# Stacking DMAs of an attention layer: rows interleaved by four, one key stack whole-width, one issued by GpSimd

## The reference

```python
def _L1_gnn_ref(x, adj_matrix, bond_matrix, Wq, bq, Wk, bk, Wv, bv, Wo, bo, seq_len):
    q, k, v = (proj(Wq, bq), proj(Wk, bk), proj(Wv, bv))
    scores = jnp.einsum('bhqd,bhkd->bhqk', q, k) * SCALE
    mask = (adj_matrix + bond_matrix)[:, None, :, :]
    scores = scores * mask
    attn = jax.nn.softmax(scores, axis=-1)
    ctx = jnp.einsum('bhqk,bhkd->bhqd', attn, v)
    ctx = ctx.transpose(0, 2, 1, 3).reshape(b, seq_len, EMBED_DIM)
    return jnp.einsum('bse,fe->bsf', ctx, Wo) + bo
```

## Time and profile before

| | |
|---|---|
| median of 3 runs | 3081.29 us (3079.47 to 3081.74) |
| the profiled execution | 3079.83 us |
| its span | 3078.0 us |
| mean granted clock of TensorE | 0.993 |
| TensorE busy | 2976.1 us (97%) |
| VectorE, ScalarE, GpSimd busy | 61%, 48%, 23% |
| DMA queue of SP | 98576 packets, 199.96 MB |

### The profile page before, as it was taken

One profiled execution on the slowest core, in us unless ns is written; L12 is line 12 of the kernel. 1 busy time (PEld: TensorE's weight loads), 2 busy tenths in 40 slices (PEclk: granted clock), 3 DMA queues, 4 the chain that ended last, 5 costly groups with the idle time before them and its releaser, 6 DMA issues.

```text
span 3078.0 us, 63372 instructions
## 1 busy us (share of the span) xinstructions
PE 2976.1 (97%) x22896; PEld 2353.4 (76%) x22896; DVE 1893.0 (61%) x4170; ACT 1473.6 (48%) x2729; POOL 692.9 (23%) x1241
## 2 busy tenths in 40 slices
PE   7999999999999999999999999999999999999999
PEld 6687786877878777788777887778867788677886
DVE  2698426984269742787437874378643786438863
ACT  1684217833178331783327833277322773238722
POOL 0243002430024300242002420034200342013410
PEclk9999999999999999999999999999999999999999
DMA  4302213022130231302313013121132212221200
GB/s 169 90 2 90 76 70 90 2 90 86 59 90 2 90 108 44 84 3 89 131 30 75 19 73 131 39 66 45 58 119 53 52 59 66 97 67 38 80 8 14
DMA packets 98905, 204.35 MB, mean 66 GB/s; under 512 B 11024, under 2 KB 42128, under 8 KB 98576
## 3 DMA queue, kind: packets, MB, share of 16 engines
q1 hardware_dynamic: 98576, 199.96, 20.9%
HBM read 136.75 MB, written 8.65 MB: 47 GB/s over the span
## 4 chain that ended last, share of the span: by engine, by line
PE 68%; issue 11%; DVE 8%; SPq 5%; POOL 4%; ACT 3%; DMA 1%; DVEq 0%; POOLq 0%; ACTq 0%
PE ps L1077 37%; PE ps L1300 11%; PE ps L1224 7%; SPq L446 4%; PE ps L1372 4%; PE ps L1252 4%; PE ps L1202 3%; POOL H L557 3%; DVE Z L787 2%; DVE stats L608 1%; DVE h L845 1%; PE ps L1114 1%; POOL nm L545 1%; ACT Z L1002 1%; DMA qS<-qlo 1%
## 5 line engine op out<-in xcount | busy, mean ns | idle before, releaser
L787 DVE CUSTOM_DVE_ANT_0 Z<-ps,adjN 128x1024 f32<-128x1024 f32 x512 | 623.8, 1218 | 69.9 <-PE ps L1202 69.9
L1002 ACT ACTIVATE Z<-Z,nm 128x1024 f32<-128x1024 f32 x512 | 587.1, 1147 | 66.7 <-POOL nm L545 66.7
L1224 PE MATMUL ps<-ident,Z 128*128 128x128 f32 x4096 | 547.8, 277 | 26.5 <-ACT Z L1002 17.6
L1224 PEld LDWEIGHTS ps<-ident,Z 128*128 128x128 f32 x4096 | 459.7, 141 | 139.3 <-issue 64.1
L1202 PE MATMUL ps<-kS,qS 128*128 128x512 f32 x1024 | 372.1, 446 | 28.4 <-DMA qS<-qlo 28.4
L534 POOL TENSOR_SCALAR ve<-mv 128x4 f32<-128x4 f32 x80 | 15.7, 196 | 1340.1 <-DVE mv L613 1339.4
L557 POOL TENSOR_SCALAR H<-adjN 128x128 fp32r<-128x128 f32 (+1 forms) x456 | 316.8, 695 | 0.0
L545 POOL TENSOR_TENSOR nm<-nm,minus 128x1 f32<-128x1 f32 x512 | 97.1, 190 | 767.4 <-DVE nm L787 762.8
L1077 PE MATMUL ps<-mh,adjT 128*128 128x256 f32 x1024 | 223.6, 379 | 0.0
L1077 PE MATMUL ps<-v,P 128*128 128x257 f32 x1024 | 223.6, 379 | 0.0
L1077 PE MATMUL ps<-hT,t3T 128*128 128x512 f32 x512 | 221.0, 592 | 0.0
(11 more groups left out here) (170 smaller groups left out, 5673.5 us busy)
## 6 DMA issues: line engine op xcount, KB each, us to landing
adjT<-adjT_in SPq DMA_DIRECT2D x8, 4096.0 KB, 13.1
adjN<-adj_in SPq DMA_DIRECT2D x8, 4096.0 KB, 17.3
adjT<-adjT_in SPq DMA_DIRECT2D x8, 2048.0 KB, 9.1
qS<-qhi SPq DMA_DIRECT2D x112, 128.0 KB, 2.5
qS<-qlo SPq DMA_DIRECT2D x112, 128.0 KB, 2.5
kS<-khi SPq DMA_DIRECT2D x96, 128.0 KB, 2.4
kS<-klo SPq DMA_DIRECT2D x96, 128.0 KB, 2.5
adjT<-adjT_in SPq DMA_DIRECT2D x8, 1536.0 KB, 12.0
```

What stands on the lines that cost most here:

```text
L787: dve.tensor_tensor_reduce(Z[:, u % ZS], ps[:, 2 * (u % 2):2 * (u % 2) + 2].rearrange("p a n -> p (a n)"), adjN[:, u // HEADS], SCORE_SCAL ...
L1002: act.activation(Z[:, u % ZS], Z[:, u % ZS], ACT.Exp, bias=nm[:, u:u + 1], accum_out=sm[:, u:u + 1]).then_inc(exps.sem, 1)
L1224: mm = pe.transpose(ps[:, turn_bank((u, s)), rows(a)], Z[:, u % ZS, rows(NT // 2 * s + a)], ident[:])
```

## The change

Three things. The rows of q and k on the partitions are interleaved: partition 4c + j of a group's tile holds column c of the group's j-th head, where it was partition 32j + c. The host permutes weights and biases accordingly, and `pick` and `stack` step by four partitions. Then k(0,2) and k(1,2) become one stack of all 1024 columns, four DMAs with one semaphore (`kS_in[0][2]`; there is none for half 1). And k(1,1) leaves SP's queue; GpSimd issues it after its addition to x, once five lower parts are there, before `negate_max(0)`. `stack` takes the issuing queue as an argument.

```diff
-        kS_in = [[signal(f"kS_in{s}{j}", 64) for j in range(HPG - 1)] for s in range(NH)]
+        kS_in = [[signal(f"kS_in{s}{j}", 64) for j in range(HPG - 1 - s)] for s in range(NH)]
...
+        def stack(queue, dst, parts, j, cols, done):
+
+            for r, src in enumerate(parts):
+                to = dst[r:P:HPG].rearrange("p (g j) n -> p g j n", j=HPG)[:, :, j, cols]
+                queue.dma_start(to.bitcast(F32), src[j:P:HPG, :, cols].bitcast(F32)).then_inc(done.sem, 16)
...
-                def stack(dst, parts, j, cols, done):
-
-                    for r, src in enumerate(parts):
-                        to = dst[HD * r:HD * r + HD].rearrange("p (g j) n -> p g j n", j=HPG)[:, :, j, cols]
-                        sp.dma_start(to.bitcast(F32), src[HD * j:HD * j + HD, :, cols].bitcast(F32)).then_inc(done.sem, 16)
-
                 def stack_k(s, j):
-                    stack(kS, (khi, khi, klo, klo), j, half(s), kS_in[s][j])
+                    stack(sp, kS, (khi, khi, klo, klo), j, half(s), kS_in[s][j])
...
                 stack_q(0, 0)
-                stack_k(1, 1)
                 stack_q(0, 1)
-                stack_k(0, 2)
-                stack_k(1, 2)
+                stack(sp, kS, (khi, khi, klo, klo), HPG - 2, slice(0, N), kS_in[0][HPG - 2])
                 stack_q(0, 2)
...
                 pool.tensor_tensor(x[:], x[:], bo1B[:].unsqueeze(1).broadcast_to([P, NT, D]), ALU.add).then_inc(xbo.sem, 1)
+                pool.wait_ge(*lo_s(b, 5))
+                stand(pool, waited_pool)
+                stack(pool, kS, (khi, khi, klo, klo), 1, half(1), kS_in[1][1])
...
-                    dve.tensor_scalar(pick[:, i, HD * r:HD * (r + 1)], ident[:, P - HD:P], float(r in blocks), None,
+                    dve.tensor_scalar(pick[:, i, r:P:HPG], ident[:, HPG - 1:P:HPG], float(r in blocks), None,
...
-                            pe.wait_ge(*kS_in[s][j](b, 64))
+                            if j < len(kS_in[s]):
+                                pe.wait_ge(*kS_in[s][j](b, 64))
...
+    def interleaved(a):
+
+        a = np.asarray(a)
+        return np.swapaxes(a.reshape(-1, P // 32, 32), -1, -2).reshape(a.shape)
...
-        "wq1": T(L1_gnn_Wq), "wk1": T(L1_gnn_Wk), "wv1": T(L1_gnn_Wv),
+        "wq1": interleaved(T(L1_gnn_Wq)), "wk1": interleaved(T(L1_gnn_Wk)), "wv1": T(L1_gnn_Wv),
...
-        "bq1": columns(L1_gnn_bq), "bk1": columns(L1_gnn_bk),
+        "bq1": columns(interleaved(L1_gnn_bq)), "bk1": columns(interleaved(L1_gnn_bk)),
```

More of the change, by code:

```diff
@@ L439, in batch @@
             def batch(b, last):
-                def stack(dst, parts, j, cols, done):
-                    for r, src in enumerate(parts):
-                        to = dst[HD * r:HD * r + HD].rearrange("p (g j) n -> p g j n", j=HPG)[:, :, j, cols]
-                        sp.dma_start(to.bitcast(F32), src[HD * j:HD * j + HD, :, cols].bitcast(F32)).then_inc(done.sem, 16)
                 def stack_k(s, j):
-                    stack(kS, (khi, khi, klo, klo), j, half(s), kS_in[s][j])
+                    stack(sp, kS, (khi, khi, klo, klo), j, half(s), kS_in[s][j])
                 def stack_q(s, j):
-                    stack(qS, (qhi, qlo, qhi, qlo), j, half(s), qS_in[s][j])
+                    stack(sp, qS, (qhi, qlo, qhi, qlo), j, half(s), qS_in[s][j])
                 sp.wait_ge(*lo_s(b, 2))
```

## The result

The changed kernel takes **3037.05 us** (median; 3035.89 to 3037.51), the kernel before 3080.85 beside it: ratio 0.9858, 95% interval 0.9841 to 0.9875. That is 43.8 us less, 5.5 us a batch, where 28.4 were forecast; the low end of the stated range was 3047. The direction was right and the size was not.

The account below looks back on a forecast made before the run. The prediction took SP's issuing queue at the head of each batch's layer 1 as the bound; removing TensorE's two waits saves 28.4 us over eight batches, 3079.8 to 3051.4, or 3053 us as a median; range 3047 to 3085.

Parts of the forecast that it names:

- Both waits: TensorE idle 1.66 us before unit 4's scores and 2.10 us before unit 6's, first batch's layer 1; both to go.
- the sum: Profiled execution 3079.8 us less 28.4 is 3051.4, or 3053 us on the scale of the median.
- Rows interleaved: Stacking DMAs touch partitions all over instead of 32 in a block; could give transfer rate, taken as no change.
- Two queues on one set of engines: GpSimd's four DMAs could make q(0,0) land about 0.55 us later; charged nothing, at most 0.6 us in one batch.
- GpSimd's price: Time of one DMA issue of k(1,1) on GpSimd: taken as 1.0 us, bounds 0.60 and 4.53 us.
- free limit of 1.36: Four GpSimd issues before unit 0's negated maximum are free up to 5.4 us in all, 1.36 us each.
- (a): GpSimd's issue is the new bound, delaying unit 0's exponential beyond 1.36 us each; 3098 us at 2.77; slower, chance 0.17.
- (b): A GpSimd issue near 1.8 us costs 1.8 us a batch, 3067 us; chance 0.10.
- The whole-width stack: Third key stack in four DMAs at 0.60 us per issue: another 2.56 us of SP's queue and unit 6's wait go.
- Rival (c): Whole-width DMA costs the queue twice or engines can't keep up: unit 6 late 1.2 us a batch, 3063 us; chance 0.08.
- Rival (e): Engines, not the queue, set the pace: unit 4's 1.66 us wait stays in every batch, 3066 us; chance 0.04.
- The range: 3047 to 3085 us; low end is 6 us under 3053, if landings shorten and the first batch's unit 2 gains.

Follow-up runs that it names:

- kept-busy run: Kernel before, with two extra matmul products that TensorE runs in unit 6's wait for the third query stack: 3066.3 us, ratio 0.9960.
- the two with extra products: Kernel before, with four or two extra matmul products run by TensorE in unit 6's wait: 3078.6 us with four, 3066.3 us with two.

## Why the prediction was right or wrong, point by point

- **What bounds the kernel.** Right: SP's queue, at two places. Both waits are gone, and with the clock full in both kernels the heads differ by 239.5 - 210.2 = 29.3 us; the sum said 28.4.
- **The term that is missing: TensorE's clock.** The sum ended with "28.4 us over the run" and priced a wait at its own length. The kept-busy run gives the rest, 13.0 us; 1.3 more lie in the set-up. Those aren't the change's, as far as the traces tell: the set-up of the kernel before took 94.9 us in its own trace and 94.4 and 93.7 in the two with extra products, which leave it as it was, and it ranges from 92.7 to 94.9 us over all 14 traces. Nor is their cause shown: in eight traces TensorE's clock falls in the set-up and in six not, and both sorts have long and short ones. 29.3 + 13.0 + 1.3 are 43.6 of the 43.9 by which the spans differ. The trace of before had the signs: a mean clock of 0.993, heads of unlike length, a value projection of 2.8 us. I read one batch in detail, the first, and wrote that "the other seven repeat it". It was the only one without half clock.
- **Rows interleaved: "I take no change for the sum".** Wrong, and the largest error of mechanism. Undone, it takes back 30 to 32 of the 44 us. By itself it moves the time little, since the queue's 0.64 us sets the pace, and that is as far as I looked; but it raises what the engines can take, and the other two parts ask for that.
- **Two queues on one set of engines: "at most 0.6 us in one batch".** Wrong for blocked rows, the case I worked out: 1.7 to 2.2 us in every batch. My own row, four DMAs as 2.3 us of extra work for the engines, was near it: in the second batch unit 2 starts 10.4 us into the head where it was 8.0. I let only 0.55 us of it reach q(0,0), since I spread GpSimd's four DMAs over 4 us at 1.0 each and took SP's issue price as fixed. They were issued in 2.4 us, together with SP's, and an issue on SP took up to 2.27 us. For interleaved rows the charge of nothing held. This error and the one above cancel in the sum: it came out near the 29.3 of the waits, but would have said the same of the blocked kernel, which gets 12 us in all. That it fits the waits so well is partly luck.
- **GpSimd's price.** 0.61 us each (2.46 for four) where I took 1.0; the free limit of 1.36 was not reached. Rivals (a) and (b) fall. (The upper bound was misread: GpSimd's longest instructions are those of L579, 4.62 us in the mean, not 4.53. Nothing but the price of rival (a) hangs on it.)
- **The whole-width stack.** The issue is 0.60 us in the median, as taken. Rival (c), the engines can't keep up, holds exactly where the rows are in blocks, with more than the price I gave it; in the changed kernel it doesn't.
- **Rival (e), the engines set the pace.** Falls: with k(1,1) back on SP the first wait returns, 1.35 us in the mean of eight, with the rows laid out as in the changed kernel.
- **The range.** Its low end allowed 6 us below the sum, for landings. A row on the clock would have put 10 to 15 us there.

## What to carry to other kernels

Price a wait of TensorE by two terms, its length and what runs at half clock behind it, and read the granted clock behind each long wait in every repetition, not in one. When DMAs are moved to a second queue or made wider, first ask at what rate the engines can take them: here a layout that gained 0.1% alone decided between 0.4% and 1.4% for the whole. And a kernel that gains from useless matmuls in a wait tells that the wait itself is worth more than it is long.

## What the hardware showed

- In the heads of the 14 traces TensorE waited 46 times for 2.0 us or more, and its clock fell to half behind 35 of these waits. Of the 25 waits of 1.5 to 1.97 us it fell behind one, of 1.74 us. So the length alone doesn't decide: the same 2.50 us did it in six batches of eight in one execution and not in the other two, and in before the first batch's 2.10 us didn't.
- From SBUF to SBUF, 32 neighbouring partitions gave 201 GB/s at a DMA share of 0.91, every fourth partition 298 at 0.83. Scaled to fully busy engines, an estimate, these are 221 and 359 GB/s.
- An issue on SP takes 0.60 us in the median whether the DMA carries 128 or 256 KB, but single ones up to 2.3 us. With rows in blocks and a second queue or a whole-width stack 34 to 56 of 352 to 384 were over 0.7 us, in the other kernels 8 to 17. That the engines hold the queue up is the reading that fits, not shown by itself.
- In the changed kernel GpSimd's issue takes 0.55 to 0.80 us, and its DMAs land in a median of 2.5 to 3.2 us, SP's of the same size in 2.1.
